# Placing every edge column by one-hot products, gathering edge ends in the loop, and unsplit fp32 weight folds

## What is computed

```python
# layer 0: row = src, col = dst
edge_feature = silu(edge_rbf @ We1 + be1) @ We2 + be2
msg = edge_feature * x[col]
agg = segment_sum(msg, row, num_segments=625)
out0 = x + (silu(agg @ Wn1 + bn1) @ Wn2 + bn2)
...
# layer 1, three times
fwd_neigh = mean_agg(h, src, dst, n) @ W_fwd[l].T
bwd_neigh = mean_agg(h, dst, src, n) @ W_bwd[l].T
h = relu(concatenate((h, fwd_neigh, bwd_neigh), axis=1) @ W_self[l].T)
```

## Time and profile before

| | us |
|---|---|
| median of 3 runs (1371.29 to 1372.97) | 1371.45 |
| the profiled execution | 1371.52 |
| its span from first to last instruction | 1369.7 |
| sort and folds, up to the first gathered edge features | 0 to 211 |
| edge loop, up to the last `flush` | 211 to 960 |
| dense layers | 960 to 1370 |

### The profile page before, as it was taken

One profiled execution on the slowest core, in us unless ns is written; L12 is line 12 of the kernel. 1 busy time (PEld: TensorE's weight loads), 2 busy tenths in 40 slices (PEclk: granted clock), 3 DMA queues, 4 the chain that ended last, 5 costly groups with the idle time before them and its releaser, 6 DMA issues.

```text
span 1369.7 us, 21273 instructions
## 1 busy us (share of the span) xinstructions
PE 1193.7 (87%) x6133; PEld 994.5 (73%) x6133; DVE 850.1 (62%) x1489; ACT 676.4 (49%) x1300; POOL 612.5 (45%) x679
## 2 busy tenths in 40 slices
PE   1488307999999999999999999999887999897867
PEld 1355206888888888888888888887867788786666
DVE  6455205777777777777777777777556343273662
ACT  2467404666666666666666666665531232222231
POOL 5888766555555555555455555552502020131110
PEclk9699657999999999999999999999998999999978
DMA  8455112222222222222222222221100101010101
GB/s 245 147 185 186 33 12 66 77 77 77 77 77 77 77 77 77 75 77 76 67 82 73 74 75 71 75 77 51 39 1 32 62 31 61 32 62 31 39 1 38
DMA packets 31131, 98.20 MB, mean 72 GB/s; under 512 B 10125, under 2 KB 10375, under 8 KB 26746
## 3 DMA queue, kind: packets, MB, share of 16 engines
q0 software_dynamic: 22592, 56.08, 14.4%
q1 hardware_dynamic: 8506, 41.67, 8.8%
HBM read 88.18 MB, written 9.42 MB: 71 GB/s over the span
## 4 chain that ended last, share of the span: by engine, by line
PE 75%; POOL 10%; DVE 7%; issue 4%; ACT 2%; DMA 1%; DVEq 0%; SPq 0%; ACTq 0%; POOLq 0%
PE ps L785 11%; PE ps L787 11%; PE ps L786 11%; POOL slots_dram L443 10%; PE ps L778 8%; PE ps L779 8%; PE ps L780 8%; PE ps L876 3%; PE ps L875 3%; PE ps L880 3%; PE ps L792 3%; PE ps L793 3%; PE ps L997 1%; PE ps L841 1%; DVE zb_lo L1461 1%
## 5 line engine op out<-in xcount | busy, mean ns | idle before, releaser
L785 PE MATMUL ps<-we_hi,s_hi 128*128 128x512 f32 x680 | 274.1, 403 | 0.0
L786 PE MATMUL ps<-we_lo,s_hi 128*128 128x512 f32 x680 | 266.5, 392 | 0.0
L787 PE MATMUL ps<-we_hi,s_lo 128*128 128x512 f32 x680 | 266.5, 392 | 0.0
L468 POOL DMA_INDIRECT xg<-h_dram,node_picks x170 | 173.0, 1018 | 98.6 <-POOL node_picks L458 67.1
L462 POOL DMA_INDIRECT rbf<-in_edge,edge_picks x170 | 189.4, 1114 | 51.7 <-issue 50.0
L615 ACT ACTIVATE m_hi<-msg 128x512 fp32r<-128x512 f32 x170 | 107.3, 631 | 166.1 <-DVE msg L1308 165.9
L1313 DVE TENSOR_TENSOR m_lo<-msg,m_hi 128x512 fp32r<-128x512 f32 x170 | 117.7, 692 | 91.0 <-ACT m_hi L615 91.0
L443 POOL DMA_INDIRECT slots_dram<-fields,row_i x111 | 141.0, 1270 | 48.0 <-issue 48.0
L541 POOL TENSOR_TENSOR w_lo<-wstage,w_hi 128x2048 fp32r<-128x2048 f32 x9 | 41.8, 4639 | 252.0 <-ACT w_hi L707 252.0
L605 ACT ACTIVATE s<-ps,be 128x256 f32<-128x256 f32 x340 | 133.9, 476 | 36.7 <-PE ps L780 36.7
L787 PEld LDWEIGHTS ps<-we_hi,s_lo 128*128 128x128 f32 x680 | 128.0, 188 | 28.2
(11 more groups left out here) (245 smaller groups left out, 2645.4 us busy)
## 6 DMA issues: line engine op xcount, KB each, us to landing
stage<-in_fold_a SPq DMA_DIRECT2D x6, 1024.0 KB, 5.6
stage<-in_fold_b SPq DMA_DIRECT2D x6, 1024.0 KB, 8.4
fold_dram<-folded SPq DMA_DIRECT2D x6, 1024.0 KB, 4.0
wstage<-fold_dram SPq DMA_DIRECT2D x6, 1024.0 KB, 4.7
w_raw<-in_nodew SPq DMA_DIRECT2D x3, 1024.0 KB, 17.4
wstage<-in_selfw SPq DMA_DIRECT2D x3, 1024.0 KB, 6.1
rbf<-in_edge,edge_picks POOLq DMA_INDIRECT x170, 2.8
xg<-h_dram,node_picks POOLq DMA_INDIRECT x170, 3.4
```

What stands on the lines that cost most here:

```text
L468: pool.indirect_dma_start(xg[t.slot][:, j], None, h_dram, bass.IndirectOffsetOnAxis(ap=node_picks[t.slot][:, j:j + 1], axis=0)).then_inc(x ...
L785: pe.matmul(outp, lh, rh, start=False, stop=False, skip_group_check=True)
L786: pe.matmul(outp, lh, rl, start=False, stop=False, skip_group_check=True)
L787: return pe.matmul(outp, ll, rh, start=False, stop=False, skip_group_check=True)
```

## The change

All 165 columns are now placed by one-hot products, in 28 groups of six columns. For a group DVE makes two one-hot tiles with one instruction each (125 x 768 and 125 x 1020, f16), ACT scales the first with a key (`mark`), PE runs six products of 170 columns (`place`), each column of a group in its own region of the accumulator. The key holds partition and group in the bits of an f16 number, the region tells the column, and DVE decodes the sum to an edge number (L1280 ff. of the new code). The indirect writes, the DRAM table and its load are gone. Source and target of an edge are packed into a DRAM array of pairs, `ends_dram`, and fetched in the loop by two more indirect DMAs for each step (8 bytes for each edge); DVE turns them into the columns for the one-hots (`edge_ends`), and `pick_nodes` takes the target from them.

The folds lose their split: `stage` is read by PE as it is, in 4 x 4 fp32 products for a fold. `stage` and `folded` have two buffers each. The groups are placed between the folds' blocks by a table `AFTER`; the last fold has none. The three node weights are split in the last three steps of the edge loop. Waits for constants are regrouped, and the two large memsets of POOL stand behind the slot computation.

```diff
-            pool.wait_ge(rows_part, 3 * C + 5)
-            for t in range(PERM, ET):
-                pool.indirect_dma_start(
-                    slots_dram, bass.IndirectOffsetOnAxis(ap=row_i[:, t:t + 1], axis=0),
-                    fields[:, t], None).then_inc(scattered[t % 5], 16)
-            pool.wait_ge(table_ready, 3)
+            pool.wait_ge(table_ready, 2)
+            pool.wait_ge(fold_mm, K * (FOLDS - 1))
...
             def pick_nodes(t):
                 t.wait(pool, msg_ready, 2, -2)
-                pool.tensor_copy(node_picks[t.slot][:], table[:, bass.ds(t.count(2), 2), 2]).then_inc(picked, 1)
+                pool.wait_ge(ends_in[t.slot], t.rounds(32))
+                pool.sem_inc(nodes_known, 1)
+                pool.tensor_copy(node_picks[t.slot][:], end_ids[t.slot][:, :, 1]).then_inc(picked, 1)
...
+                for j in range(2):
+                    pool.indirect_dma_start(
+                        end_ids[t.slot][:, j], None, ends_dram,
+                        bass.IndirectOffsetOnAxis(ap=edge_picks[t.slot][:, j, 1:2], axis=0)).then_inc(ends_in[t.slot], 16)
...
+            def place(i):
+                pe.wait_ge(hots_hi_made, i + 1)
+                pe.wait_ge(marks_made, i + 1)
+                r = i % HOT_RING
+                for j in range(min(GROUP, ET - i * GROUP)):
+                    mm = pe.matmul(ps[:, 5 + j // 2, j % 2 * REGION:j % 2 * REGION + TILES],
+                                   marked[r][:, j // 2, :, j % 2], hot_hi[r][:, j // 2, :, j % 2],
+                                   start=False, stop=False, skip_group_check=True)
+                mm.then_inc(perm_mm, 1)
+            def fold(m, u):
+                f = slice(u * P, u * P + P)
+                pe.wait_ge(stage_in[m % 2], 32 * (m // 2 + 1))
+                if m > 0:
+                    pe.wait_ge(fold_ev, (m - 1) * K + u + 1)
+                for k in range(K):
+                    mm = pe.matmul(ps[:, 1 + u], stage[m % 2][:, 0, k, f], stage[m % 2][:, 1, k],
+                                   start=k == 0, stop=k == K - 1)
+                mm.then_inc(fold_mm, 1)
...
+            def edge_ends(t):
+                s = t.slot
+                dve.wait_ge(ends_in[s], t.rounds(32))
+                t.wait(dve, hots_ready, 3, -3)
+                dve.tensor_tensor(ends[s][:], end_ids[s][:], base2[:, bass.ds(t.count(2), 2)],
+                                  op=ALU.subtract).then_inc(ends_ready, 1)
...
                 if t.reg is not None or t.c + 2 < STEPS:
                     rows_lo(t.at(2))
+                    edge_ends(t.at(2))
                 message_lo(t, 0)
                 message(t, 1)
+                if t.reg is None and t.c >= STEPS - 3:
+                    weights_low(t.c - STEPS + 5, t.c - STEPS + 6)
```

More of the change, by code:

```diff
@@ L70 @@
 EPS = 1e-5
-def each(eng, n, body):
-    body(0)
-    with eng.Fori(1, n) as m:
-        body(m)
-def wait_rounds(eng, sem, m, per, add=0):
-    if not isinstance(m, int) or m * per + add > 0:
-        eng.wait_ge(sem, m * per + add)
 class Step:
@@ L830, in _ @@
[L830 to L834 removed]
+            pe.matmul(ps[:, 0, 8:8 + C], ones32[0:EP, :], counts32[:], start=True, stop=True).then_inc(rank_mm, 1)
+            def place(i):
[7 more added lines that the diff above has]
+                mm.then_inc(perm_mm, 1)
@@ L837, in turn_rows @@
+            for m in range(FOLDS):
+                for u in range(K):
+                    fold(m, u)
+                    for i in AFTER[m][u]:
+                        place(i)
             def turn_rows(t):
```

496 lines of the change are left out of this document (254 added, 242 removed).

## The result

| | before | after | ratio, 95% interval |
|---|---|---|---|
| median of the runs, us | 1371.74 (1371.29 to 1372.97) | 1415.89 (1398.30 to 1431.54) | 1.024 (1.016 to 1.033) |
| profiled execution, us | 1371.52 | 1398.30 | |

Forecast were 1312 us and a range from 1282 to 1352. The changed kernel was slower than before. Its runs also spread over 33 us, where those of before spread over 1.7. Three of the four runs of before in this table are the ones given with its profile above.

A forecast was written before the change was run, and what follows sets the result against it. POOL's writes were taken to bound the first stage and PE the loop, with POOL just over PE's pace after the change: 1371.5 - 94.4 - 2 + 27.5 + 9 = 1312 us, range 1282 to 1352.

The forecast's parts named there:

- Part 1: First stage: without POOL's writes PE sets its end; the loop's first product at 118.4 instead of 212.77, 94.4 us less.
- The feeders: First stage: DVE's two one-hot instructions take 2.2 us a group at most, ACT's about 0.85; both stay under PE.
- rival 5: First stage: fp32 work held at 1.2 GHz, 84.5 + 16.5 us again, 1412 us in all; chance 4%.
- rival 3: First stage: fp32 fold products cheap at 0.45 us each, 41 us less, 1271 us in all; chance 4%.
- Part 2: Edge loop: two more gathers make POOL's step 9.04 us, over PE's 8.67; 27.5 us more.
- rival 1: Edge loop: POOL stays hidden under PE's 8.67 us step, the 27.5 us vanish, 1284 us in all; chance 15%.
- rival 4: Edge loop: contention stretches each new gather to 2.20 + 0.30 us, 217 us more, 1500 us in all; chance 4%.
- Part 3: End of the loop: three weight splits moved into the last three steps cost 9 us more, ends 4 and 14.
- The 2 us for the clock: Start of the loop: its clock was 0.50 until 225 us; PE now comes from dense work, 2 us less.

The follow-up runs named there:

- e11: The changed kernel run again, unedited, in another set than the result's: 1290.57 us, ratio 0.942.
- set A: The set of the result itself, before and the changed kernel together on one chip: 1371.74 and 1415.89 us, ratio 1.024.
- e7: The changed kernel with one new gather of end_ids a step instead of two, the other half fixed numbers: 1291.09 us, ratio 0.941.
- e5: Before with two more 8-byte-row gathers a step, at fixed row numbers, that no other engine waits for: 1392.59 us, ratio 1.014.
- e9: e5 with the real index edge_picks for its small gathers and POOL's wait for earlier gathers moved ahead of pick_edges: 1391.11 us, ratio 1.015.
- e10: e9 with the changed kernel's waits on the two small gathers added: 1384.88 us, ratio 1.011.
- e4: Before with only its folds' products made unsplit fp32, the splits still made and waited for: 1375.48 us, ratio 1.003.
- e6: Before with two POOL memsets of 128 x 1400 fp32 added a step and no added gather: 1395.57 us, ratio 1.017.
- set E: A later set with the unedited changed kernel and its version with one new gather a step, on one chip: 1359.80 and 1292.51 us.
- e3: The changed kernel with the two end_ids gathers replaced by SP's plain DMAs of fixed rows, same bytes and waits: 1304.18 us, ratio 0.952.
- e13: e7 again, the changed kernel with one new gather a step, beside e12 on one chip: 1292.51 us, ratio 0.943.
- e12: The changed kernel a third time, unedited: 1359.80 us, ratio 0.990.
- D: The set in which the unedited changed kernel ran again as e11, beside e9 and e10: 1290.57 us for e11.
- e16: Before with three of PE's signals a step given 1.4 to 2.1 us late on purpose: 1374.50 us, ratio 1.003.

## Why the prediction failed, step by step

The terms of the sum are held against e11, since nothing comes late in it, and against the recorded run.

**Part 1, the first stage: right in its mechanism, 6 us too careful.** PE of the changed kernel in set A, at the start, between two fold halves and at the stage's end:

```profile
9.58 0.55 PE L821 MATMUL ps<-counts,before 125*125 125x5 f32 x2 [9.58 <-DVE counts L1204]
10.42 4.61 PE L841 MATMUL ps<-stage 128*128 128x512 f32 x5
...
29.48 3.63 PE L841 MATMUL ps<-stage 128*128 128x512 f32 x8
32.94 1.09 PE L830 MATMUL ps<-hot_hi,marked 125*128 125x170 f16 x12
33.88 2.34 PE L841 MATMUL ps<-stage 128*128 128x512 f32 x5
...
93.47 17.36 PE L841 MATMUL ps<-stage 128*128 128x512 f32 x40
110.67 0.27 PE L857 MATMUL ps<-ident,rbf 128*128 128x128 f32 x1
```

PE starts the folds at 10.42 (forecast 10.8) and ends them at 110.7 (115.4). A row's x counts instructions, and an fp32 product of 512 columns shows as two: x8 from 29.48 to 32.94 is four products, 0.865 us each (forecast 0.88). Twelve placement products of 170 columns lie between 32.94 and 33.88, 0.078 us each (0.94 / 12), where I took 0.10. By the distances between starts all 165 took 13.8 us and the folds 86.4, PE's waits among them; forecast were 16.5, 84.5 and 3.6 for waits and clock. The start is slow: up to 15.68 the folds' instructions stand 0.85 us apart, later ones 0.43, although the clock row shows 1.00 there. The feeders, priced from `m_lo` and `s_lo` in the earlier trace rows, were cheaper too:

```profile
43.12 0.55 DVE L1242 TENSOR_TENSOR hot_lo<-iota_lo,lo 125x768 f16<-125x768 f16 x1
43.59 0.68 DVE L1242 TENSOR_TENSOR hot_hi<-iota_hi,hi 125x1020 f16<-125x1020 f16 x1
```

768 and 1020 elements took 0.55 and 0.68 us, where 0.96 and 1.22 were taken from fp32 rows: one-hots of f16 cost little over half, and PE waited for the groups in three places only, 1.0 us in all. The clock was 1.00 from 10 to 112 us, so rival 5 (half clock, 1412) didn't occur, nor rival 3 (cheap fp32, 1271). First product of the loop: 112.41 in e11, 100.4 us earlier than before (forecast 94.4), and 113.58 in set A.

**Part 2, the loop: the step that failed.** The sum had one way for the gathers to cost, POOL's own time: 9.04 us a step, 27.5 us. Two things were wrong.

First, its size. POOL of e11, a step of the loop:

```profile
602.61 0.19 POOL L470 COPY node_picks<-end_ids 128x2 int32<-128x2 int32 x1
603.58 1.06 POOL L484 DMA_INDIRECT xg<-h_dram,node_picks  x1 [0.79 <-POOL node_picks L470]
...
608.96 0.95 POOL L478 DMA_INDIRECT end_ids<-ends_dram,edge_picks  x1 [0.30 <-DVE msg L1329]
610.21 0.94 POOL L478 DMA_INDIRECT end_ids<-ends_dram,edge_picks  x1 [0.30 <-issue]
611.29 0.18 POOL L470 COPY node_picks<-end_ids 128x2 int32<-128x2 int32 x1
...
620.14 0.18 POOL L470 COPY node_picks<-end_ids 128x2 int32<-128x2 int32 x1
```

From pick to pick 8.68 and then 8.85 us, 8.76 on average, which is PE's step. POOL has no wait in it but the 0.79 for its own copy and the 0.30 between gathers, so it is full and just keeps up. That PE sets the 8.76 shows in e7, which has one gather less and the same step, and where POOL does wait for `msg`:

```profile
600.13 0.18 POOL L474 COPY node_picks<-end_ids 128x2 int32<-128x2 int32 x1 [1.19 <-DVE msg L1333]
```

I took 1.06 + 0.30 for a new gather, the mean of both kinds in the loop; the small ones took 0.95 + 0.30, and those of `rbf` 1.04 on average between 300 and 840 us instead of 1.11. That is the outcome of rival 1, which I gave 15%, at 1284: e11 took 1290.6. The step of e5 and e9 (8.91 and 8.89), where the gathers are behind before's order and unwaited for, was nearer to 9.04. So an excess exists where the order leaves it. In e10, with the changed kernel's order and waits, it is 8.763.

Second, a mechanism that had no term. With six gathers a step, PE's signals reach ACT and DVE late in some sets, and in set A the loop is 109 us longer than in e11 (874.6 against 765.5). Why they are late stays open. I had a case of contention, rival 4, but put it on the length of a gather (2.20 us): gathers took 0.98 to 1.03 us in set A. Its price, 217 us in the loop, was too high and its place was wrong. The rule of the Trainium skill that is cited there (SBUF — State Buffer, Who interferes with whom) doesn't show in the new gathers either, which were to be no cheaper than the mean of 1.06: they took 984 ns on average in the worse set and 948 in the better.

**Part 3, the end of the loop: right.** DVE of e11:

```profile
848.17 2.29 DVE L1250 TENSOR_TENSOR w_lo<-w_raw,w_hi 128x2048 fp32r<-128x2048 f32 x1 [3.02 <-ACT w_hi L580]
...
860.03 2.29 DVE L1250 TENSOR_TENSOR w_lo<-w_raw,w_hi 128x2048 fp32r<-128x2048 f32 x1 [3.02 <-ACT w_hi L580]
...
877.12 0.81 DVE L1358 TENSOR_TENSOR acc_adj<-ps,acc_adj 125x626 f32 x1 [0.36 <-PE ps L898]
```

Each split holds DVE for 3.02 + 2.29 us, where I had 4.9. From the last transposes to the end of the last addition it is 36.7 us in e11 and 24.3 before: 12.4 more, forecast 9 (4 to 14).

**The sum again, with e11.** 1371.5 - 100.4 (first stage) + 7 (PE's step of 8.760 against 8.674, over 82 steps) + 12.4 (end of the loop) - 1 (rest of the loop) - 2.6 (dense stages) = 1287, and the profiled execution has a span of 1284.9 and some 2 us around it. The 7 us come from second-layer products: within a half of the layer they stand 0.2373 us apart on average instead of 0.2331. All kernels of the changed family have this, and before with extra gathers (e5, e9) too; e4 and e6 don't. Its cause I leave open.

**The 2 us for the clock.** Windows of e11 at the start of the loop:

```profile
112.00:140.00 28.00, 24.36 (x121) 20.66 (x122) 14.65 (x28) 17.86 (x35) 19.34 (x24) 0.88 0.60 223
125.00:140.00 15.00, 15.00 (x81) 12.51 (x80) 10.35 (x21) 10.61 (x22) 9.44 (x13) 1.00 0.25 75
```

The clock is 1.00 and PE full from 125 us on, where before it was 0.50 until 225. What this gave lies in the 1 us of the loop's rest.

**The chances.** 0.91 for faster rested on a list of cases that all took the loop's engines to hand over their work as they did before. The trace of before could not show what two more gathers a step would do to PE's signals, which in it are never late. What could have been seen is that no case had a term for the time from one engine to another. That in the better sets the kernel lands 21 us below the 1312, near rival 1, doesn't make the forecast right: the part of it that failed in set A, the handover, is in none of its terms.

## What to carry to other kernels

Where a change adds indirect gathers to a loop that has some already, price two things: POOL's own time, and what late signals would cost. Read in the waits how much a result may come late before the engine behind it stalls. Run such a kernel in several sets on different chips before its time is believed: here one program took 1291, 1360 and 1416 us (medians), and before stood still each time, so a steady reference proves nothing for the kernel beside it. Of the versions tried, none that does the whole work was faster than the changed kernel at its best (1290.6 us, 0.942 of before); in set A it lost (1.024) and in set E it was within 1% of before (0.990), so before, with four gathers a step, is the steadier one of the two.

## What the runs showed of the hardware that I had not expected

- A semaphore update of TensorE can stand 7 us and more behind the start of its product (498.03 to 505.43), in sets whose traces list about half of the updates, while those of ACT, DVE and POOL stand 0.01 us behind their instructions. With four gathers a step nothing was lost by it in e3 (80 us of late starts, the step of e2), nor with five in e13 (44 us, 1293 us); six took 67 us more than five in set E (e12 against e13) and 125 more in set A than in D (against e11).
- An indirect gather of 128 rows of 8 bytes held POOL for 0.95 us on average in e11, one of 512 or 2048-byte rows for 1.05 to 1.06: the price is that of the gather, hardly that of its bytes.
- An fp32 product of 512 columns took 0.865 us at a granted clock of 1.00 (29.48 to 32.94 of set A), and shows as two instructions.
- Three signals a step given 1.4 to 2.1 us late cost before 3 us of 1372 (e16).
